# Row maxima of causal attention: the mask added by DVE while it takes the maxima, with partial maxima as seeds of the next ones

## The reference, cut to what matters

```python
# B, T, D = 4, 1024, 128; 16 heads of 64; x: (4, 1024, 128) fp32
q, k, v = x @ wq.T, x @ wk.T, x @ wv.T            # of the layer-normed x, split into heads
q, k = apply_rotary_emb(q, cos, sin), apply_rotary_emb(k, cos, sin)
scores = jnp.einsum('bhid,bhjd->bhij', q, k) * scale
scores = jnp.where(causal, scores, -jnp.inf)
probs = jax.nn.softmax(scores, axis=-1)
out = jnp.einsum('bhij,bhjd->bhid', probs, v)     # then @ wo.T
x = x + layernorm(attention(layernorm(x)))
x = x + layernorm(ffn(layernorm(x)))              # ffn: linear, SwiGLU, 8 experts (top 4) + shared, linear, SwiGLU
```

## Time and profile before

| | |
|---|---|
| median of 3 runs | 1261.14 us (1259.26 to 1264.67) |
| profiled execution | 1261.32 us |
| its span, first to last instruction | 1259.3 us |
| mean granted TensorE clock | 0.975 |
| PE / DVE / ACT / POOL busy | 91% / 78% / 76% / 75% of the span |
| products with maskN (line 438) | 512 |
| reductions of maxima (lines 703 and 699) | 384 + 192 |

### The profile page before, as it was taken

One profiled execution on the slowest core, in us unless ns is written; L12 is line 12 of the kernel. 1 busy time (PEld: TensorE's weight loads), 2 busy tenths in 40 slices (PEclk: granted clock), 3 DMA queues, 4 the chain that ended last, 5 costly groups with the idle time before them and its releaser, 6 DMA issues. The chain is left out here.

```text
span 1259.3 us, 34888 instructions
## 1 busy us (share of the span) xinstructions
PE 1144.7 (91%) x13543; PEld 788.8 (63%) x13543; DVE 983.3 (78%) x2220; ACT 956.5 (76%) x2193; POOL 947.3 (75%) x984
## 2 busy tenths in 40 slices
PE   4689999999999999999999999999999598999996
PEld 1256676676767676767667676767777454566553
DVE  7798777787868797878778787979674559867987
ACT  3667888878787878787887879787979665766574
POOL 3578889889888989898988889898767475334463
PEclk8699999999999999999999999999999899999998
DMA  6652425243351515152515334251602100000011
GB/s 201 147 135 52 123 65 129 60 118 82 89 127 43 133 38 136 37 134 69 129 49 128 83 87 118 53 135 35 153 2 65 51 2 1 1 1 1 2 35 34
DMA packets 50660, 97.03 MB, mean 77 GB/s; under 512 B 6720, under 2 KB 23360, under 8 KB 48448
## 3 DMA queue, kind: packets, MB, share of 16 engines
q1 hardware_dynamic: 50496, 94.81, 30.2%
HBM read 58.47 MB, written 34.60 MB: 74 GB/s over the span
## 5 line engine op out<-in xcount | busy, mean ns | idle before, releaser
L807 POOL TENSOR_TENSOR Plo<-P,Phi 128x512 f16<-128x512 f32 (+3 forms) x640 | 538.3, 866 | 129.2 <-ACT P L498 128.6
L495 ACT ACTIVATE Phi<-psS 128x512 f16<-128x512 f32 (+3 forms) x768 | 384.0, 500 | 149.5 <-PE psS L353 105.9
L498 ACT ACTIVATE P<-psS 128x512 f32<-128x512 f32 (+3 forms) x640 | 307.0, 480 | 0.0
L347 PE MATMUL psS<-Q,K 128*128 128x512 f16 (+3 forms) x768 | 252.0, 328 | 40.5 <-DVE Plo L654 37.1
L374 PE MATMUL psO<-V,Plo 128*128 128x65 f16 x2304 | 288.7, 194 | 0.0
L370 PE MATMUL psO<-V,Phi 128*128 128x65 f16 x2304 | 287.5, 192 | 0.0
L372 PE MATMUL psO<-V,Phi 128*128 128x64 f16 x2304 | 286.6, 192 | 0.0
L703 DVE TENSOR_REDUCE pmax<-psX 128x1 f32<-128x512 f32 x384 | 252.9, 684 | 23.0 <-PE psX L434 14.3
L370 PEld LDWEIGHTS psO<-V,Phi 128*128 128x128 f16 x2304 | 219.5, 98 | 56.6 <-issue 0.4
L350 PE MATMUL psS<-Q,K 65*128 65x512 f16 (+3 forms) x768 | 252.2, 328 | 0.0
L434 PE MATMUL psX<-K,Q 128*128 128x512 f16 (+4 forms) x768 | 227.5, 332 | 11.7 <-DMA Q<-HL 3.8
(11 more groups left out here) (200 smaller groups left out, 2161.1 us busy)
## 6 DMA issues: line engine op xcount, KB each, us to landing
K<-k_way SPq DMA_DIRECT2D x48, 512.0 KB, 7.0
k_way<-HL SPq DMA_DIRECT2D x64, 256.0 KB, 3.7
q_way<-HL SPq DMA_DIRECT2D x60, 256.0 KB, 3.7
Q<-q_way SPq DMA_DIRECT2D x60, 256.0 KB, 7.1
Q<-q_way SPq DMA_DIRECT2D x15, 512.0 KB, 11.9
out<-y SPq DMA_DIRECT2D x8, 256.0 KB, 2.2
y<-in_x SPq DMA_DIRECT2D x3, 512.0 KB, 10.8
hn<-in_x SPq DMA_DIRECT2D x3, 512.0 KB, 5.5
```

The source lines that it names most:

```text
L347: nc.tensor.matmul(out, M.K1[:, p, h, j * P:(j + 1) * P], M.Q1[:, p, h, c:c + w], start=True, stop=False)
L495: nc.scalar.activation(M.Phi[:, U % NP_, 0:w], X, ACT.Exp, scale=SCALE)
L498: nc.scalar.activation(full, X, ACT.Exp, scale=SCALE).then_inc(S.exp_done, 1)
L807: nc.gpsimd.tensor_tensor(M.Plo[:, U % NP_, 0:w], M.P32[:, U % NP_, 0:w], M.Phi[:, U % NP_, 0:w], ALU.subtract).then_inc(S.lo_pool, 1)
```

## The change

The nine banks are ordered anew, so that the plain ones come first. PE makes no product with `maskN`. For a piece that doesn't touch the diagonal, DVE takes a plain maximum straight into `rmax`. For a piece that ends on the diagonal, it does one instruction that adds the mask (zero but for the last 128 columns) to the piece, writes the sum back into the PSUM bank, and folds its maximum with a start value into `rmax`: with the lowest number if the piece starts at key tile 0, with the partial maximum of key tiles 0 to 3 if it starts at tile 4. A head so has 12 instructions in place of 9: 4 plain reductions and 8 of the new kind, 4 of these seeded. The joins go, with `pmax` and `pmix`. One mask of 128x512 replaces the two of 128x128; for the scores, mask and identity change places in the product of line 353. "mt" moves from step 43 to 42.

```diff
@@ -65,9 +65,8 @@
 
-MAXB = [[(2, 0, 3), (0, 0, 1)], [(6, 4, 3), (4, 4, 1)], [(1, 0, 2), (5, 4, 2)],
-        [(3, 0, 4)], [(4, 0, 4)], [(5, 0, 4)], [(6, 0, 4)], [(7, 0, 4)], [(7, 4, 4)]]
-NMIX = 3
+MAXB = [[(4, 0, 4)], [(5, 0, 4)], [(6, 0, 4)], [(7, 0, 4)], [(7, 4, 4)],
+        [(3, 0, 4)], [(2, 0, 3), (0, 0, 1)], [(6, 4, 3), (4, 4, 1)], [(1, 0, 2), (5, 4, 2)]]
 assert sorted((t, j + i) for bank in MAXB for t, j, n in bank for i in range(n)) == [
@@ -83,15 +82,14 @@
 LN_STEPS = (23, 30)
-MX_FIRST, MX_LAST, JOIN_STEP, MT_STEP = 8, 39, 40, 43
+MX_FIRST, MX_LAST, MT_STEP = 8, 39, 42
 TR1_STEPS, WO_STEPS, TR0_STEPS = (11, 15), (19, 21), (32, 36)
...
 MX_FIRST_GROUP = ((-1, 7), (-1, 20), (0, 0), (0, 8))
-JOIN_FIRST = ((-1, 15), (-1, 28), (0, 8), (0, 16))
 MT_FIRST = ((-1, 17), (0, 1), (0, 11), (0, 19))
-MX_SECOND, JOIN_SECOND, MT_SECOND = (13, 41), 42, 44
+MX_SECOND, MT_SECOND = (13, 41), 44
 EARLY_STEPS = 12
@@ -350,7 +348,7 @@
                 if diagonal:
-                    mm = nc.tensor.matmul(out[:, 0:P], M.ident16[:], M.maskT[:], start=False, stop=True)
+                    mm = nc.tensor.matmul(out[:, 0:P], M.mask[:, BANK - P:BANK], M.ident16[:], start=False, stop=True)
                 mm.then_inc(S.scores_ready, 1)
@@ -430,19 +428,16 @@
                     for t, j, n in MAXB[k]:
-                        diagonal = j + n - 1 == t
                         mm = nc.tensor.matmul(X[:, c:c + n * P], M.Q1[0:rows, p, h, t * P:(t + 1) * P],
-                                              M.K1[0:rows, p, h, j * P:(j + n) * P], start=True, stop=not diagonal)
+                                              M.K1[0:rows, p, h, j * P:(j + n) * P], start=True, stop=True)
                         c += n * P
-                        if diagonal:
-                            mm = nc.tensor.matmul(X[:, c - P:c], M.ident16[:], M.maskN[:], start=False, stop=True)
                 elif kind == "mt":
...
                         h = a[0]
-                        pe.wait_ge(S.row_max, h + 1)
+                        taken(pe, (s, "mx", h, len(MAXB) - 1))
                         mm = nc.tensor.transpose(X[0:TT, 0:P], M.rmax[:, h * TT:(h + 1) * TT], M.ident[:])
                     else:
-                        pe.wait_ge(S.row_max, s + 1 + GH)
+                        taken(pe, (s, "mx", GH - 1, len(MAXB) - 1))
                         mm = nc.tensor.transpose(X[0:GH * TT, 0:P], M.rmax[:], M.ident[:])
@@ -695,13 +690,26 @@
                     ready(dve, item)
-                    if k < NMIX:
-                        nc.vector.tensor_reduce(M.pmix[:, h, k, :], X.rearrange("p (j i) -> p j i", i=P), AX.X,
-                                                ALU.max).then_inc(free(item), 1)
-                    else:
-                        t, j, _ = MAXB[k][0]
-                        nc.vector.tensor_reduce(M.pmax[:, int(j > 0), h, t:t + 1], X, AX.X,
-                                                ALU.max).then_inc(free(item), 1)
+                    if s < 0 and h == 0 and k == 0:
+                        dve.wait_ge(S.consts, 2)
+                    if k == 0 and s == 0:
+                        ready(dve, (-1, "mt", h))
+                    if k == 0 and h == 0 and s > 0:
+                        ready(dve, (s - 1, "mt"))
+                    c = 0
+                    for t, j, n in MAXB[k]:
+                        own = M.rmax[:, h * TT + t:h * TT + t + 1]
+                        part = X[:, c:c + n * P]
+                        c += n * P
+                        if j + n - 1 < t:
+                            last = nc.vector.tensor_reduce(own, part, AX.X, ALU.max)
+                        else:
+                            if j > 0:
+                                taken(dve, (s, "mx", h, MAXB.index([(t, 0, 4)])))
+                            last = nc.vector.tensor_tensor_reduce(
+                                out=part, in0=part, in1=M.mask[:, BANK - n * P:BANK], scale=1.0,
+                                scalar=own if j > 0 else LOWEST, op0=ALU.add, op1=ALU.max, accum_out=own)
+                    last.then_inc(free(item), 1)
                 elif kind == "wo":
@@ -712,35 +720,6 @@
                         nc.vector.tensor_tensor(y, X, y, ALU.add).then_inc(free(item), 1)
-
-            def join_head(h):
-
-                last = (-1, "mx", h, len(MAXB) - 1)
-                for k in range(NAUX):
-                    dve.wait_ge(S.aux_free[(number[last] - k) % NAUX], (number[last] - k) // NAUX + 1)
-                if h == 0:
-                    dve.wait_ge(S.consts, 3)
-                nc.vector.tensor_reduce(M.pmax[:, 1, h, 2:7:4], M.pmix[:, h, 0:2, 0:3], AX.X, ALU.max)
-                nc.vector.tensor_reduce(M.pmax[:, 1, h, 1:6:4], M.pmix[:, h, 2, :].rearrange("p (g j) -> p g j", j=2),
-                                        AX.X, ALU.max)
-                nc.vector.tensor_copy(M.pmax[:, 1, h, 0:5:4], M.pmix[:, h, 0:2, 3]).then_inc(S.max_parts, 1)
-                dve.wait_ge(S.max_parts, h + 1)
-                nc.vector.tensor_reduce(M.rmax[:, h * TT:(h + 1) * TT], M.pmax[:, :, h, :].rearrange("p a t -> p t a"),
-                                        AX.X, ALU.max).then_inc(S.row_max, 1)
-
-            def join_max(s):
-
-                last = (s, "mx", GH - 1, len(MAXB) - 1)
-                for k in range(NAUX):
-                    dve.wait_ge(S.aux_free[(number[last] - k) % NAUX], (number[last] - k) // NAUX + 1)
-                nc.vector.tensor_reduce(M.pmax[:, 1, :, 2:7:4], M.pmix[:, :, 0:2, 0:3], AX.X, ALU.max)
-                nc.vector.tensor_reduce(M.pmax[:, 1, :, 1:6:4],
-                                        M.pmix[:, :, 2, :].rearrange("p h (g j) -> p h g j", j=2), AX.X, ALU.max)
-                nc.vector.tensor_copy(M.pmax[:, 1, :, 0:5:4], M.pmix[:, :, 0:2, 3]).then_inc(S.max_parts, 1)
-                dve.wait_ge(S.max_parts, s + 1 + GH)
-                ready(dve, (s - 1, "mt") if s else (-1, "mt", GH - 1))
-                nc.vector.tensor_reduce(M.rmax[:], M.pmax[:].rearrange("p a h t -> p (h t) a"), AX.X,
-                                        ALU.max).then_inc(S.row_max, 1)
 
@@ -788,10 +767,6 @@
                     side(item)
-                if (s, u) in JOIN_FIRST:
-                    join_head(JOIN_FIRST.index((s, u)))
-                if ((s, "mt") in number) and u == (JOIN_STEP if s > 0 else JOIN_SECOND):
-                    join_max(s)
                 if s >= 0 and U <= last_unit and not lo_on_pool(U % SU):
@@ -830,21 +805,18 @@
             nc.gpsimd.memset(M.ident16[:], 0.0)
-            nc.gpsimd.memset(M.maskT[:], 0.0)
-            nc.gpsimd.memset(M.maskN[:], 0.0).then_inc(S.consts, 1)
+            nc.gpsimd.memset(M.mask[:], 0.0).then_inc(S.consts, 1)
             pool.wait_ge(S.consts, 1)
...
 
-            nc.gpsimd.affine_select(out=M.maskT[:], in_=M.maskT[:], compare_op=ALU.is_ge, fill=NEG, base=0,
-                                    pattern=[[1, P]], channel_multiplier=-1)
-            nc.gpsimd.affine_select(out=M.maskN[:], in_=M.maskN[:], compare_op=ALU.is_ge,
+            diagonal = M.mask[:, BANK - P:BANK]
+            nc.gpsimd.affine_select(out=diagonal, in_=diagonal, compare_op=ALU.is_ge,
                                     fill=NEG, base=0, pattern=[[-1, P]], channel_multiplier=1).then_inc(S.consts, 1)
...
             nc.gpsimd.memset(M.eps[:], EPS)
-            nc.gpsimd.memset(M.V[:, :, :, :, 2 * HD:2 * HD + 1].rearrange("p a t h o -> p (a t h) o"), 1.0)
-            nc.gpsimd.memset(M.pmax[:], LOWEST).then_inc(S.consts, 1)
+            nc.gpsimd.memset(M.V[:, :, :, :, 2 * HD:2 * HD + 1].rearrange("p a t h o -> p (a t h) o"), 1.0).then_inc(S.consts, 1)
             pool.wait_ge(S.w_hi, 1)
@@ -994,13 +966,10 @@
         M.ident16 = sb(stack, "ident16", [P, P], BF16)
-        M.maskT = sb(stack, "maskT", [P, P], BF16)
-        M.maskN = sb(stack, "maskN", [P, P], BF16)
+        M.mask = sb(stack, "mask", [P, BANK], BF16)
         M.x_tiles = I["x"].rearrange("b (t p) d -> p (b t) d", p=P)
...
         M.V = sb(stack, "V", [P, 2, TT, GH, VW], F16)
-        M.pmax = sb(stack, "pmax", [P, 2, GH, TT], F32)
-        M.pmix = sb(stack, "pmix", [P, GH, NMIX, BANK // P], F32)
         M.xT = sb(stack, "xT", [P, 2, 2, T], F16)
```

More of the change, by code:

```diff
@@ L1805, in build @@
         S.v_hi = sem("v_hi")
-        S.max_parts = sem("max_parts")
-        S.row_max = sem("row_max")
         S.k_out = sem("k_out")
```

## The result

The changed kernel takes 1265.89 us (median of 15 runs, 1264.18 to 1269.36), the kernel before 1260.04 (15 runs). The ratio is 1.0048 with an interval of 1.0037 to 1.0059: slower by 5.9 us, half a per cent, as surely as it is small. The profiled execution took 1266.84 us, its span is 1264.8.

A forecast was written before the change was run, and what follows sets the result against it. PE was taken to set the pace in steps 12 to 26, where it has no gap, and DVE's queue elsewhere. +7 us over 14 groups, +2 and +0.5 made 1261.3 + 9.5 = 1270.8, say 1270 us; range 1243 to 1292.

The forecast's parts named there:

- rival 2: Whole kernel: PE's saving and DVE's additions of about 3.5 us per group cancel, 1258 to 1267 us; chance 0.22.
- Additions on DVE: Maxima on DVE: starts, read-outs, seeds and a wait add 1.13 us per head, 4.5 us per group.
- The starts: Three banks read in two pieces: three more DVE instructions per head at 0.07 us each, 0.21 us.
- the seeds: Four maxima per head take their start value from memory: 0.06 us each, 0.24 us per head.
- The read-outs: Reading out the maximum of the eight new DVE instructions per head: 0.07 us each, 0.56 us.
- The wait: Once per head DVE must let the instruction that makes the seed end first: 0.12 us.
- By stretch, group 11: Group cut by steps: gains and losses from DVE's additions, PE's saving and the join sum to +0.5 us per group.
- The join: Ahead of the remainder at a group's end: 1.15 us on DVE; without it PE waits 0.5 us less per group.
- The earlier transposition: One step earlier, costed at nothing; its DMA to Q2, waited for 1.9 us in twelve groups, might come late.
- PE's saving: 512 mask products at 0.057 us, 29 us: 0.2 of 0.9 us kept in steps 12 to 26, nothing in 27 to 37.
- Outside the groups 1 to 14: Group 0, carrying half its own maxima besides the next group's: +2 us; before it, one head and a join: +0.5.
- Rival 3: DVE's maxima: read-outs cost what ACT's do, +3.4 us per group, up to 1315 us; chance 0.12.

The follow-up runs named there:

- e11: The kernel before, with each of the three mixed banks reduced in two instructions in place of one: 1265.41 us, ratio 1.0037.
- e4: The kernel before, with the join of the maxima moved behind the remainder DVE makes in the same step 40: 1261.19 us, ratio 1.0007.
- e8: The changed kernel with the transposition of the maxima put back to step 43: 1267.71 us, ratio 1.0069 of before.
- e1: The kernel before without PE's 512 mask products for the maxima, DVE and joins as before: 1249.14 us, ratio 0.9918.
- e10: The kernel before without mask products for the maxima and with the transposition in step 42 in place of 43: 1246.61 us, ratio 0.9893.
- e2: The kernel before with one more 24-column reduction on DVE ahead of each of the 576 reductions of maxima: 1280.72 us, ratio 1.0163.
- e3: The changed kernel with bank (7, 0, 4) first, which parts the seed from its use: 1261.92 us, ratio 1.0016 of before.
- e7: The changed kernel with the banks reordered: (7,0,4) first, split banks 2nd, 5th and 8th, (7,4,4) 7th: 1265.67 us, ratio 1.0047.

## Why the prediction came out as it did

The direction was right, and so was the place, steps 27 to 37: forecast +9.5 us for the profiled execution, measured +5.5 in its span, and 1265.9 us for the runs against 1270. The time lies in the range. It does not lie in the forecast's own part of it, which began at 1268, but in the band of rival 2 (1258 to 1267), and its 5.9 us are under the 6.3 us that I had set as the border of "it cancels", chance 0.22. Rival 2's premise, additions of about 3.5 us per group, is also nearer to the 2.9 measured than my 4.5. And part of the hit is luck: three terms were off, two of them against the third. Point by point:

- **Additions on DVE**: 1.13 us per head forecast, 0.72 measured on average. The starts were nearly right (0.21; 3 x 0.06 in e11), the seeds too (0.24; 0.07 at 512 columns, 0.06 at 384, 0.02 each at 256 and 128, together 0.17). The read-outs are the term that was mis-sized most: 0.56 forecast, 0.24 measured, as most of the read hides. It is a second instruction, as the Trainium skill states (VectorE: DVE Perf Modes, Two Vector instructions with no wait between them). The trace agrees, with a row of 0.14 us, and yet it is all but free behind a long instruction. The wait was 0.12 forecast and is 0.23 where it is paid; since that is in 34 of 64 heads, the average is 0.12 again, by luck. The joins' row from which I took it waits for a plain instruction's end, the seed's wait comes on top of a pointer operand; the trace doesn't part these.
- **Writing back into PSUM and the column rate at nothing**: right, 0.61 against 0.60 us.
- **By stretch, group 11**: steps 12 to 26 forecast -0.2, measured -0.2; steps 27 to 37 +1.0, measured +0.8; steps 8 to 11 +0.2, measured +0.1; the rest -0.5, measured -0.2. The sum was +0.5. It is +0.5 in group 11, and +0.38 on average from group 1 to 14, 5.3 us.
- **The join**: the step that failed. I had given its going 0.5 us per group, 7 us in all. e4 shows that the wait behind it is ACT's: moved out of the way it gives nothing. I had also misread its length. The three maxima in front of it do not start 0.60 us apart, the last one starts at 769.42, so DVE could go on at 770.02, and the join with its waits is 0.95 us, not 1.15. The 0.60 itself is right; a row of two maxima 3 us earlier has it (1.28 us for two of 0.68):

```profile
765.11 1.28 DVE L703 TENSOR_REDUCE pmax<-psX 128x1 f32<-128x512 f32 x2
```
```profile
769.42 0.69 DVE L703 TENSOR_REDUCE pmax<-psX 128x1 f32<-128x512 f32 x1
```

- **The earlier transposition**: costed at nothing, worth 1.8 us (e8; 2.5 from e1 to e10). The term was on my page: the 1.9 us in which PE waited for the row of maxima. I feared that it would grow, and it went.
- **PE's saving**: that it pays in steps 12 to 26 and hardly behind them is what e1 shows (21.9 to 21.2, 12.9 to 12.9). By itself it is worth 10.7 us.
- **Outside the groups 1 to 14**: before group 0 +0.5, as forecast. Group 0 forecast +2, measured -0.9: it lies from 61.7 to 130.7 us before and from 62.2 to 130.3 after. Behind group 14 +0.6 us, where no maxima are made; that is within what the second phase varies by from one execution to the next (e4's is 1.0 us longer than that of the kernel before, with the same code there).
- **Two slips without effect**: in the earlier trace rows three matmuls have 128 columns, not four; their starts do lie 0.057 us apart. Rival 3's own terms give +1.2 and +1.9 us in its two stretches, where it has +1.0 and +2.0.

So the account of the change reads: PE's products -10.7 us (e1), the earlier transposition -1.8 (e8), the joins nothing (argued from e4), and DVE's additions 46 us, of which e2's price of 0.40 makes 18.5. That is +6.0; +5.9 is measured. So close a match is partly luck, since the three prices measured for DVE's time are 0.40 (e2), 0.48 (e11) and 0.5 (e3), and the order of the banks alone moves up to 4 us (e7). The charge for the read-outs and the seeds by themselves was not measured.

## What to carry to other kernels

When two engines are both nearly full, cut the loop into stretches and ask of each which engine has no gap: work moved from one to the other can be gained in one stretch and lost in the next, and the two don't cancel. A saving on PE was worth about 0.4 of its time here, an addition on DVE was charged 0.4 to 0.5, so moving work from PE to DVE pays only if it costs DVE less time than it saves PE (29 us saved against 46 added). Before work is made cheaper, ask whether it is needed: dropping the mask gave more than any place to put it.

## What the runs showed that was not expected

- DVE's read-out of an accumulator has a row of 0.14 us, but the next instruction starts with it: against a plain reduction the masked one with its read-out delays the next start by 0.01 us at 384 or 512 columns and by 0.05 us at 128 or 256.
- A DVE instruction that waits for its predecessor's result and takes it as a scalar starts 0.83 us after a 512-column reduction, where without the wait it is 0.60: 0.23 us for one semaphore, twice what the join's first instruction paid. Where other DVE work lies between the two, no such gap is left (30 of 64 heads).
- A gap that ends with work can hide a second wait behind it: the join seemed to hold up the remainder by about 1 us, and moving it away gave 0.
- A wait can grow without costing time: in e8 PE waited 2.4 us more for the remainder, and the groups were as long as before.
